# Feed-forward of layer 0: two of four hidden chunks get their outer convolution taps from VectorE, ScalarE and GpSimd in place of TensorE

## What is computed

```python
def bit_linear(x, w):                 # act_quant: rows to integers in -128..127 and back
    return einsum('bsd,hd->bsh', act_quant(x), weight_quant(w))   # weight_quant: -1, 0, 1 times a scale

h = bit_linear(layernorm(x), w1)      # 128 -> 512
h = depthwise_conv1d(h.transpose(0, 2, 1), conv_w, conv_b)   # 3 taps over the tokens, padding 1
h = silu(h.transpose(0, 2, 1))
x = x + bit_linear(h, w2)             # 512 -> 128, h is quantised again first
```

## Time and profile before

| | us |
|---|---|
| median of 3 runs | 563.39 |
| lowest and highest of them | 557.45, 567.11 |
| profiled execution, its own time | 562.17 |
| its span, first to last instruction | 560.4 |
| busy in the span: TensorE matmul | 476.8 |
| VectorE | 338.8 |
| ScalarE | 310.4 |
| GpSimd | 222.9 |

### The profile page before, as it was taken

How to read it: one execution, slowest core, us unless ns; L and a number is a source line. 1 busy time by engine, 2 the same in 40 slices (tenths; PEclk the granted TensorE clock), 3 DMA queues, 4 the chain that set the end, 5 groups by cost and what they waited for, 6 DMA issues and landing times.

```text
span 560.4 us, 12414 instructions
## 1 busy us (share of the span) xinstructions
PE 476.8 (85%) x3906; PEld 394.6 (70%) x3906; DVE 338.8 (60%) x1238; ACT 310.4 (55%) x676; POOL 222.9 (40%) x456
## 2 busy tenths in 40 slices
PE   3389898999998899958899999998999897499970
PEld 1277666776765788947877777776777597489970
DVE  6777677877782157677677787786868243022203
ACT  3137666777766445655866755665556563155540
POOL 7963322122313124445000125345254467745550
PEclk9989999999999999977999999999999998699995
DMA  6613333333407970034533333332210201322107
GB/s 177 191 43 110 90 115 105 111 92 95 125 3 303 424 235 2 10 119 136 172 120 97 92 106 118 103 111 83 92 55 8 74 20 34 91 66 70 49 15 225
DMA packets 52266, 60.05 MB, mean 107 GB/s; under 512 B 7633, under 2 KB 43354, under 8 KB 50928
## 3 DMA queue, kind: packets, MB, share of 16 engines
q1 hardware_dynamic: 46672, 52.73, 30.1%
q0 software_dynamic: 2272, 4.24, 2.3%
q10 hardware_dynamic: 3264, 2.36, 1.4%
HBM read 30.01 MB, written 29.23 MB: 106 GB/s over the span
## 4 chain that ended last, share of the span: by engine, by line
PE 51%; DVE 5%; DMA 4%; issue 3%; another core or an unknown queue 3%; ACT 2%; POOL 1%; DVEq 0%; SPq 0%; POOLq 0%
PE ps L1690 6%; PE ps L1639 6%; PE ps L1730 6%; PE ps L1733 5%; PE ps L1879 5%; PE ps L1889 5%; PE ps L1651 3%; PE ps L1653 2%; PE ps L1652 2%; ACT probs L996 1%; PE ps L1624 1%; DMA k_blocks<-y_dram 1%; PE ps L1940 1%; PE ps L1857 1%
## 5 line engine op out<-in xcount | busy, mean ns | idle before, releaser
L996 ACT ACTIVATE probs<-ps 128x512 f32<-128x512 f32 x256 | 147.4, 597 | 79.4 <-PE ps L1733 73.7
L1639 PE MATMUL ps<-k_blocks,q_stacks 128*128 128x256 f32 x512 | 118.5, 315 | 12.5 <-DMA k_blocks<-k_dram 6.6
L1268 DVE CUSTOM_DVE_ANT_0 ps<-ps,mask_q 128x256 f32<-128x256 f32 x256 | 102.5, 452 | 36.4 <-PE ps L1639 35.4
L1733 PE MATMUL ps<-q_stacks,k_blocks 128*128 128x256 f32 x512 | 105.3, 289 | 0.9 <-DMA q_stacks<-maxT 0.8
L1733 PEld LDWEIGHTS ps<-q_stacks,k_blocks 128*128 128x128 f32 x512 | 86.8, 189 | 20.8 <-issue 10.8
L1292 DVE TENSOR_REDUCE row_max<-ps 128x2 f32<-128x512 f32 x128 | 84.3, 687 | 27.5 <-PE ps L1639 26.2
L1639 PEld LDWEIGHTS ps<-k_blocks,q_stacks 128*128 128x128 f32 x512 | 80.2, 195 | 18.6 <-DMA k_blocks<-k_dram 5.3
L1690 PE MATMUL ps<-probs,v_aug 128*32 128x256 f32 x1024 | 68.5, 385 | 5.5 <-ACT probs L996 3.7
L796 POOL TENSOR_SCALAR max_split<-row_max 128x16 fp32r<-128x16 f32 x32 | 6.5, 204 | 156.7 <-issue 66.7
L1730 PE MATMUL ps<-mask_k,neg_mask_eye 128*128 128x512 f32 x128 | 54.5, 426 | 0.6 <-ACT experts L902 0.5
L741 POOL DMA_INDIRECT y_dram<-x_ring x39 | 40.8, 1046 | 28.4 <-ACT x_ring L1078 20.3
(11 more groups left out here) (221 smaller groups left out, 828.3 us busy)
## 6 DMA issues: line engine op xcount, KB each, us to landing
slots_dram<-x_ring SPq DMA_DIRECT2D x1, 10400.0 KB, 28.8
q_stacks<-q_dram SPq DMA_DIRECT2D x32, 256.0 KB
q_dram<-qk_parts SPq DMA_DIRECT2D x16, 384.0 KB, 3.7
k_dram<-qk_parts SPq DMA_DIRECT2D x16, 384.0 KB, 4.0
k_blocks<-k_dram SPq DMA_DIRECT2D x128, 48.0 KB
x_ring<-slots_dram SPq DMA_DIRECT2D x39, 65.0 KB
ctx_in<-ctx SPq DMA_DIRECT2D x16, 128.0 KB, 2.2
mask_in<-mask_Bx1xSxS_ik SPq DMA_DIRECT2D x8, 256.0 KB, 2.8
```

The source lines that it names most:

```text
L996: eng.activation(probs[:, n // HPS % 2, n % HPS, :, :].rearrange("p k q -> p (k q)"), ps[:, head_bank(BANKS_T, n)[0], :], ACT.Exp).then_in ...
L1268: last = eng.tensor_tensor_reduce(out=scored, in0=scored, in1=mask_q[t % 2][:, i, :], scale=1.0, scalar=-3.0e38, op0=ALU.add, op1=ALU.max, ...
L1639: mm = eng.matmul(ps[:, bank, i * S:(i + 1) * S], q_stack[r][:, st, i * P:(i + 1) * P], k_blocks[r][:, st, j, :], start=True, stop=True)
L1733: mm = eng.matmul(ps[:, bank, k * S:(k + 1) * S], k_blocks[r][:, st, j, k * P:(k + 1) * P], q_stack[r][:, st, :], start=(l == 0), stop=(l ...
```

## The change

For chunks 2 and 3 TensorE makes the middle product alone, with weights into which no tap is folded. Chunk 2 gets the middle tap by a scaled copy on ScalarE (`conv_middle`) and the outer taps by two multiply-and-adds on VectorE, straight from PSUM (`conv_sides`). Chunk 3 gets three scaled copies on ScalarE, one for each tap, and two additions on GpSimd (`conv_whole`). The SiLU is parted in two: chunks 0 and 1 as before, chunks 2 and 3 from SBUF behind both. The copies lie in the end of the `experts` tile, which is written only after the stage. On each engine:

- TensorE: chunks 2 and 3 of `ffn_hidden` have one product each, not three.
- ScalarE: `conv_middle` ahead of the first half of the SiLU, the second half behind `rounding(b)`.
- VectorE: `conv_sides(b+1)` between `quant_scale(b)` and `quant_clip(b)`.
- GpSimd: `conv_whole(0)` and `conv_whole(1)` between the last body of layer 0's attention and the tail; `conv_whole(b+2)` ahead of `ln_power(b)` in the loop.

Some semaphores are merged as well (`bo_ps`, `bo_new` and `x_biased` to `bo_sum`; `f_mean` into `f_stat`), with the same order of work; `h_act` counts two for each batch. The diff, cut to its core:

```diff
+    TAPPED = 2
+        conv_out = experts[:, E * EW - 4 * S:].rearrange("p (r c t) -> p r c t", r=2, c=2)
+        conv_side = experts[:, E * EW - 8 * S:E * EW - 4 * S].rearrange("p (r k t) -> p r k t", r=2, k=2)
...
+        def conv_whole(eng, b, r):
+
+            eng.wait_ge(h_mid, b + 1)
+            out, side = conv_out[:, r, 1, :], conv_side[:, r, :, :]
+            eng.tensor_tensor(out[:, 1:S], side[:, 0, 0:S - 1], out[:, 1:S], ALU.add).then_inc(h_side, 1)
+            eng.wait_ge(h_side, b * 2 + 1)
+            eng.tensor_tensor(out[:, 0:S - 1], side[:, 1, 1:S], out[:, 0:S - 1], ALU.add).then_inc(h_side, 1)
...
+            eng.tensor_copy(w1_taps[:, 1, TAPPED:FC, :], ffn_raw[:, 0, TAPPED:FC, :])
             for k in range(3):
-                for c in range(FC):
+                for c in range(TAPPED):
                     last = eng.tensor_scalar(w1_taps[:, k, c, :], ffn_raw[:, 0, c, :], conv_w[:, c, k:k + 1], None, ALU.mult)
...
             attention_gpsimd(eng, 0, "main 0", {-1: add_output_bias, 0: routing_constants})
+            conv_whole(eng, 0, 0)
+            conv_whole(eng, 1, 1)
             attention_gpsimd(eng, 0, "tail")
             attention_gpsimd(eng, 1, "head")
             for b in range(NB):
+                if exists(b + 2):
+                    conv_whole(eng, b + 2, b % 2)
                 ln_power(eng, ln_f0, b)
                 ln_apply(eng, ln_f0, b, bo[1])
...
+        def conv_middle(eng, b, r):
+
+            eng.wait_ge(h_ps, b * 2 + 2)
+            if after(b, 1):
+                eng.wait_ge(h_act, 2 * (b - 1))
+            eng.activation(conv_out[:, r, 0, :], hidden_ps(r, 2), ACT.Copy, scale=conv_w[:, 2, 1:2])
+            for k in range(2):
+                eng.activation(conv_side[:, r, k, :], hidden_ps(r, 3), ACT.Copy, scale=conv_w[:, 3, 2 * k:2 * k + 1])
+            eng.activation(conv_out[:, r, 1, :], hidden_ps(r, 3), ACT.Copy, scale=conv_w[:, 3, 1:2]).then_inc(h_mid, 1)
+
+        def conv_sides(eng, b, r):
+
+            eng.wait_ge(h_mid, b + 1)
+            chunks = (2,)
+            for c in chunks:
+                out, h = conv_out[:, r, c - 2, :], hidden_ps(r, c)
+                last = eng.scalar_tensor_tensor(out=out[:, 1:S], in0=h[:, 0:S - 1], scalar=conv_w[:, c, 0:1], in1=out[:, 1:S],
+                                                op0=ALU.mult, op1=ALU.add)
+            last.then_inc(h_conv, 1)
+            eng.wait_ge(h_conv, b * 2 + 1)
+            for c in chunks:
+                out, h = conv_out[:, r, c - 2, :], hidden_ps(r, c)
+                last = eng.scalar_tensor_tensor(out=out[:, 0:S - 1], in0=h[:, 1:S], scalar=conv_w[:, c, 2:3], in1=out[:, 0:S - 1],
+                                                op0=ALU.mult, op1=ALU.add)
+            last.then_inc(h_conv, 1)
+
+        def ffn_silu(eng, b, r, half):
             if after(b, 0):
                 eng.wait_ge(g_ps, b * NT)
-            for c in range(FC):
-                eng.wait_ge(h_ps, b * 2 + c // 2 + 1)
-                last = eng.activation(f_act[:, c, :], hidden_ps(r, c), ACT.Silu, bias=conv_b[:, c:c + 1])
+            if half == 0:
+                eng.wait_ge(h_ps, b * 2 + 1)
+                for c in range(TAPPED):
+                    last = eng.activation(f_act[:, c, :], hidden_ps(r, c), ACT.Silu, bias=conv_b[:, c:c + 1])
+            else:
+                eng.wait_ge(h_conv, b * 2 + 2)
+                eng.wait_ge(h_side, b * 2 + 2)
+                for c in range(TAPPED, FC):
+                    last = eng.activation(f_act[:, c, :], conv_out[:, r, c - TAPPED, :], ACT.Silu, bias=conv_b[:, c:c + 1])
             last.then_inc(h_act, 1)
...
                     if l == 0 and isinstance(b, int) and b == NB and n == 5:
                         eng.wait_ge(a.pv, NB * 4 - 1)
-                        ffn_silu(eng, 0, 0)
+                        conv_middle(eng, 0, 0)
+                        ffn_silu(eng, 0, 0, 0)
+                    if l == 0 and isinstance(b, int) and b == NB and n == 10:
+                        ffn_silu(eng, 0, 0, 1)
...
             def step(b, r):
                 if exists(b + 1):
-                    ffn_silu(eng, b + 1, 1 - r)
+                    conv_middle(eng, b + 1, 1 - r)
+                    ffn_silu(eng, b + 1, 1 - r, 0)
                 if exists(b - 1):
                     int_copy(b - 1)
                 if exists(b):
                     rounding(b)
+                if exists(b + 1):
+                    ffn_silu(eng, b + 1, 1 - r, 1)
                 if exists(b - 2):
                     xT_copy(b - 2)
...
+                    if l == 0 and isinstance(b, int) and b == NB and n == 6:
+                        conv_sides(eng, 0, 0)
...
+                quant_scale(b)
+                if exists(b + 1):
+                    conv_sides(eng, b + 1, 1 - r)
+                quant_clip(b)
...
             for c in range(2 * half, 2 * half + 2):
                 h = hidden_ps(r, c)
-                eng.matmul(h[:, :], w1T[:, 1, c, :], x, start=True, stop=False)
-                eng.matmul(h[:, 1:S], w1T[:, 0, c, :], x[:, 0:S - 1], start=False, stop=False)
-                mm = eng.matmul(h[:, 0:S - 1], w1T[:, 2, c, :], x[:, 1:S], start=False, stop=True)
+                if c >= TAPPED:
+                    mm = eng.matmul(h[:, :], w1T[:, 1, c, :], x, start=True, stop=True)
+                else:
+                    eng.matmul(h[:, :], w1T[:, 1, c, :], x, start=True, stop=False)
+                    eng.matmul(h[:, 1:S], w1T[:, 0, c, :], x[:, 0:S - 1], start=False, stop=False)
+                    mm = eng.matmul(h[:, 0:S - 1], w1T[:, 2, c, :], x[:, 1:S], start=False, stop=True)
...
-                for c in range(FC):
+                for c in range(TAPPED if k in (0, 2) else FC):
                     mm = eng.transpose(ps[:, bank, c * P:(c + 1) * P], w[:, c, :], ident[:, :])
...
-                eng.wait_ge(h_act, b + 1)
+                eng.wait_ge(h_act, 2 * (b + 1))
```

More of the change, by code:

```diff
@@ L332, in build @@
         h_ps, h_act = sem("h_ps"), sem("h_act")
+        h_mid, h_conv = sem("h_mid"), sem("h_conv")
+        h_side = sem("h_side")
         g_ps, g_stat, g_round, g_int = sem("g_ps"), sem("g_stat"), sem("g_round"), sem("g_int")
@@ L856, in add_output_bias @@
                 eng.wait_ge(ln_pre.xn, 3)
-                eng.wait_ge(bo_new, 2)
+                eng.wait_ge(bo_sum, 4)
                 eng.tensor_tensor(x_res[:, :, :], x_res[:, :, :],
-                                  bo[0][:, None, :].to_broadcast([P, NB * NT, D]), ALU.add).then_inc(x_biased, 1)
+                                  bo[0][:, None, :].to_broadcast([P, NB * NT, D]), ALU.add).then_inc(bo_sum, 1)
             def routing_constants():
@@ L1143, in ffn_scalar @@
             ffn_steps(eng, step, {1: lambda: attention_scalar(eng, 0, "tail")})
-            ffn_silu(eng, NB - 2, 0)
+            conv_middle(eng, NB - 2, 0)
+            ffn_silu(eng, NB - 2, 0, 0)
             int_copy(NB - 4)
@@ L1151, in ffn_scalar @@
             xT_copy(NB - 5)
-            ffn_silu(eng, NB - 1, 1)
+            conv_middle(eng, NB - 1, 1)
+            ffn_silu(eng, NB - 1, 1, 0)
             int_copy(NB - 3)
             rounding(NB - 2)
+            ffn_silu(eng, NB - 1, 1, 1)
             xT_copy(NB - 4)
@@ L1567, in _ @@
             eng.tensor_copy(ident_bf[:, :], ident[:, :])
-            eng.wait_ge(bo_ps, 2)
+            eng.wait_ge(bo_sum, 2)
             eng.wait_ge(bias_loaded, 6 * DMA)
             for l in range(2):
-                eng.tensor_tensor(bo[l][:, :], ps[:, BANKS_PRE["bo"], l * D:(l + 1) * D], bo[l][:, :], ALU.add).then_inc(bo_new, 1)
+                eng.tensor_tensor(bo[l][:, :], ps[:, BANKS_PRE["bo"], l * D:(l + 1) * D], bo[l][:, :], ALU.add).then_inc(bo_sum, 1)
             attention_vector(eng, 0, "main 0")
@@ L2084, in _ @@
             eng.wait_ge(f_stat, 2)
-            eng.matmul(ps[:, BANKS_PRE["mean"], 0:2], mean_ones[:, :], wq_stat[:, 0:2], start=True, stop=True).then_inc(f_mean, 1)
+            eng.matmul(ps[:, BANKS_PRE["mean"], 0:2], mean_ones[:, :], wq_stat[:, 0:2], start=True, stop=True).then_inc(f_stat, 1)
             eng.wait_ge(ln_pre.xn, 2)
@@ L2099, in _ @@
                 eng.matmul(ps[:, BANKS_PRE["bo"], l * D:(l + 1) * D], bv_wide[:, l, :], wo[l][:, :],
-                           start=True, stop=True).then_inc(bo_ps, 1)
+                           start=True, stop=True).then_inc(bo_sum, 1)
             eng.wait_ge(ln_pre.xs, 5)
```

27 lines of the change are left out of this document (11 added, 16 removed).

## The result

Six runs of the changed kernel have a median of 571.83 us (569.91 to 573.19), six of the kernel before 562.49; the ratio is 1.0174, 95% interval 1.0142 to 1.0205.

| runs | changed, us | before, us | ratio, 95% interval |
|---|---|---|---|
| first | 571.83 | 562.49 | 1.0174 [1.0142, 1.0205] |
| e7 | 570.87 | 562.40 | 1.0174 [1.0133, 1.0214] |
| e9 | 569.27 | 562.05 | 1.0131 [1.0085, 1.0178] |
| e15 | 569.39 | 563.39 | 1.0111 [1.0072, 1.0150] |

The account below looks back on a forecast made before the run. TensorE was taken to bound the feed-forward stage. From 562.17 us, plus 3.6 of lateness at the stage's end, less 0.3 in the prologue, came 565.5; one more clock fall of 0.8 made 566.3 us, range 560 to 571 (0.50).

Parts of the forecast that it names:

- What bounds the kernel: Feed-forward stage: TensorE is the bound, busy 7.00 of 7.00 us; the other engines have about 2 to 3 us of room.
- The start: Start of the feed-forward: batch 0's SiLU transposes 3.6 us late, because conv_whole(0) queues on GpSimd behind batch 7's ln_power.
- The clock behind the gap: Behind the 5.1 us TensorE idle stretch at the start: half clock for some 4 us, costing 1.7 us on the path.
- The tail: quantise_rows(7) stands behind conv_whole(1) on GpSimd, takes 3.0 us; batch 2's transposes come 3.3 us late.
- The steady steps: Feed-forward loop: first step 8.7 us, next two 14.1 together; 22.8 for three against 21.6 before, +1.2.
- one more fall: TensorE's idle pieces within the feed-forward steps bring one further drop to half clock, costing 0.8 us.
- Rival D: Feed-forward steps: the clock falls in most of them, 1.3 us a step, +6, 572.3 us; chance 0.12.
- Crowding: Feed-forward steps: VectorE's clips and GpSimd's work slow each other when side by side; 0.3 us allowed in the two-step loop.
- The end of the stage: Batch 5's lateness of 4.5, less 1.7, plus 0.8: low_parts 3.6 us late, and nothing behind gives that back.
- rival E: End of the feed-forward: no lateness reaches the end, since scores and experts' loads wait for transfers anyway; 562 us, chance 0.11.
- Rival B: Feed-forward steps: TensorE's relief counts, GpSimd's additions finish before wanted, ScalarE bounds steps at 6.0 us; 557.4 us, chance 0.13.
- Rival C: Feed-forward: GpSimd becomes the bound outright, additions 1.5 us each; +6, 572.3 us, chance 0.14.

Follow-up runs that it names:

- e7: The changed kernel run again, unaltered, beside the kernel before: 570.87 us against 562.40, ratio 1.0174.
- e9: The changed kernel run again, unaltered, as yardstick for runs beside it: 569.27 us against 562.05 for the kernel before, ratio 1.0131.
- e15: The changed kernel run once more, unaltered, as yardstick: 569.39 us against 563.39 for the kernel before, ratio 1.0111.
- e5: Against the kernel before: only chunk 3's outer taps moved to VectorE, three chunks kept as TensorE products, nothing on GpSimd; 558.79 us against 562.40, ratio 0.9953.
- e12: The changed kernel with GpSimd's first pair of additions moved ahead of batch 7's LayerNorm power: 565.27 us, ratio to the kernel before 1.0076.
- e11: The kernel before plus two pairs of GpSimd additions on spare memory, awaited by batches 0 and 1's SiLU: 568.76 us against 562.05, ratio 1.0104.
- e4: The changed kernel with TensorE's 5 us gap filled by repeating batch 6's row transposes 18 times: 570.60 us, ratio to the kernel before 1.0090.
- e10: The changed kernel with the start gap and the steps' gaps on TensorE filled by needless transposes: 567.39 us, ratio to the kernel before 1.0093.
- e1: The changed kernel with all of GpSimd's additions moved to VectorE: 563.02 us against 563.96 for the kernel before, ratio 0.9941.
- e3: The kernel before with 48 extra transposes (5.2 us) holding TensorE ahead of the first SiLU transposes: 569.32 us against 563.96, ratio 1.0086.
- e6: Against the kernel before: only chunk 3's taps moved to ScalarE copies and GpSimd additions, nothing new on VectorE; 567.23 us, ratio 1.0111.
- e2: The changed kernel with only batches 0 and 1's additions moved from GpSimd to VectorE: 564.71 us, ratio to the kernel before 1.0017.
- e13: The changed kernel with GpSimd's first pair of additions moved earlier and the steps' gaps filled by needless transposes: ratio to the kernel before 1.0008.

## Why the prediction came out half

Two steps of the prediction failed. It took 14.1 us for the two-step loop and 0.8 for all further falls of the clock, and the traces have 14.4 to 15.3 for that loop; with the tail this is 1.4 us. And it put what lies behind the stage at nothing ("nothing behind gives the 3.6 back"), where the profiles differ by 2.8 us, the cause of which stays open. The parts in order:

**What bounds the kernel: right.** TensorE was the bound of the stage before, and e5 shows what relief is worth while it stays so: its steps are shorter by the products that are gone.

**The start: right.** The place behind `ln_power` of batch 7 delayed the first transposes by 3.5 us (forecast 3.6), by way of a gap of 5.0 (5.1). e12 moves that pair alone and the lateness goes; e11 brings it into the kernel before and it comes. That it fits so well is in part luck: the first pair took 1.42 us from start to end where 1.8 were taken, and the hand-over and the SiLU behind it 1.0 where 0.8 were.

**The clock behind the gap: right.** 1.7 us, by e4 too. The clock was at half until 202.7, longer than the "some 4 us", but the work on the path meanwhile was the 1.7 us of the forecast. The Trainium skill ("TensorE: Matmul & The Clock Gate", HAM oscillation) has idle gaps cost the rate of the work behind them; the trace agrees with it at 196 us, and e10, where transposes to no purpose keep the clock at 1.00, shows it in the other direction.

**The tail: 0.7 short, 0.9 with what had come before it.** `quantise_rows` took 3.5 us, from 203.73 to 207.2, not 3.0; that is most of it.

**The steady steps: mis-sized, and over other work than forecast.** The step that failed is the sum's "14.1" for the two-step loop and, with it, the "one more fall" of 0.8. The first of the three steps came as forecast, 8.69 us (222.04 less 213.35; forecast 8.7). The two behind it took 15.32 (237.36 less 222.04); in the four profiles 15.3, 14.4, 15.3, 14.4. The forecast led the loop from the SiLU over the transposes (0.45) and VectorE's maxima and factors (1.9) to the rounding, and counted ScalarE's queue as a loop by itself (5.6). In e7, one of the shorter two, the chain is ScalarE's queue in that place: the copy of the rows, the change's four copies, the first SiLU half and the integer copy, 3.4 us and not 2.35.

```profile
221.84 0.27 ACT xnT_all L1182
222.10 0.36 ACT experts L913
...
224.29 0.97 ACT f_intT L1177 x2
225.27 1.17 ACT probs L1170 x2
```

LayerNorm was longer there as well (3.97 for 3.65), the additions shorter (1.65 for 1.8). The forecast's allowances, 0.5 for hand-overs and 0.6 for crowding and `conv_sides`, hid most of this, so that 14.1 came near 14.4 was in part luck. The two longer ones have a fall to half clock near their start, here from 223 to 226 us, behind an idle stretch of 2.98, and there the chain is TensorE's: its integer transposes and first product took 0.84 and 0.96 us in the chain above, and 0.45 and 0.49 at full clock two batches later.

```profile
223.00:224.00 1.00, 1.00 (x11) 1.00 (x9) 1.00 (x2) 1.00 (x4) 0.90 (x2) 0.51 0.00 0
...
226.00:227.00 1.00, 1.00 (x5) 0.84 (x4) 0.89 (x2) 0.57 (x1) 0.92 (x2) 0.78 0.00 0
```

So 0.3 of the 1.2 too little was the loop itself and 0.9 the fall, which the forecast had counted apart, at 0.8. Each of the four profiles has one or two such falls between 205 and 240 us, and not every gap brings one: e7's begins at 207 behind 1.43 us of idle time, and behind its 3.04 us at 218.8 the clock stays at 1.00; the same 1.43 us brought none in the profile above. The forecast's comparison with a single stretch could not tell which gap would bring one. The kernel before has no fall there in two profiles, and both kernels have falls behind 245. Rival D (falls in most steps) therefore fell. By e10 to `low_parts`, 60.0 us from the first product against 62.3 to 63.8 in the four profiles, all new falls together cost 2.3 to 3.8 us; the forecast had 1.7 and 0.8 for them.

**Crowding: right in kind.** The two clips stretch beside GpSimd's work. From the groups of VectorE's instructions between 190 and 245 us (line, tiles, count, busy us, mean ns): kernel before, changed kernel, and e1, where GpSimd does no additions.

```profile
L1475 DVE TENSOR_SCALAR f_int<-probs 128x512 bf16<-128x512 f32 x12 | 5.0, 461 | 0.0
```

```profile
L1536 DVE TENSOR_SCALAR f_int<-probs 128x512 bf16<-128x512 f32 x12 | 6.6, 586 | 0.0
```

```profile
L1533 DVE TENSOR_SCALAR f_int<-probs 128x512 bf16<-128x512 f32 x14 | 5.3, 417 | 0.0
```

One such clip of 128x512 takes 0.42 us undisturbed and up to 0.95 beside GpSimd's two-input additions: in the changed kernel the four clips of 0.85 to 0.95 us all ran beside L455, L768 or L770, while two beside the one-input instructions of `quantise_rows` took 0.42 and 0.52 (one-input work is not always harmless: in e5 a clip beside the mask conversion L784 took 0.85). In e1 no clip is stretched, but VectorE's own second addition (L770) takes 0.93 to 0.95 us the four times that it runs beside L455, and 0.42 the other four. The Trainium skill ("SBUF — State Buffer", SBUF: two separate sides) states a pair of ports that GpSimd shares with VectorE, where VectorE works in a two-port mode or with two inputs in SBUF, and that one instruction holds whole while the other waits. The doubling of single instructions, in place of a small slowing of all, agrees with it, but no run here shows in which mode the clip works, nor separates the port from other causes.

**The end of the stage: right.** It gave back 1.2 us between batch 5's transposes and `low_parts`, forecast 0.9, and from there nothing (rival E was wrong, as e3 shows).

**Behind the stage: 2.8 us that no step had, the largest piece of the error.** The sum stopped at the end of the stage ("nothing behind gives the 3.6 back"); that something behind could take more was not in it. Lateness alone does not do that: e3's 5.2 us cost 4.8. One difference is seen in the second half of the experts, where the clock is at half for longer in this profile (window of 17 us from about the same place: before, changed, and e9, the same kernel in another run):

```profile
481.00:498.00 17.00, 11.68 (x73) 10.97 (x73) 1.91 (x5) 4.45 (x13) 9.27 (x10) 0.70 0.30 82
```

```profile
487.00:504.00 17.00, 11.74 (x56) 11.17 (x57) 1.11 (x3) 3.50 (x11) 8.11 (x9) 0.53 0.26 71
```

```profile
487.00:504.00 17.00, 12.10 (x66) 11.65 (x67) 1.71 (x4) 4.32 (x12) 9.40 (x10) 0.70 0.30 77
```

In e9 the clock is as before, so the change doesn't force the fall; and e9's stretch from the first masked product to the end is 287.8 us, hardly less than the 288.0 of the profile with the lower clock, so this window doesn't explain the 2.8 us either. That stretch took 285.2 and 287.0 us in two profiles of the kernel before and 286.2 in e11; in the changed kernel 288.0, 290.0, 287.8 and 288.3; in the variants 286.1 (e6), 287.7 (e2), 288.7 (e10), 289.5 (e12), 290.6 (e4), and in e1, e5 and e13, whose stages are among the shortest, 291.3, 290.7 and 291.0. These are single executions, and some lie over the median of their kernel: e5's profile is of a run of 564.24 us, 5.4 over its median, which alone could cover its long stretch. So that the changed kernel is longer there than the kernel before, in all four profiles, is measured, its code being the same; why is open, and so is how much of it is the draw of the profiled run. Even the start of the stage, 183.1, 182.6, 182.1 and 181.7 us in the changed kernel, was 185.6 in e4, which has the same code up to there. The stage is the measure here that repeats best, to 1.2 and 1.4 us within each kernel.

**The account.** Of the 9.3 us by the first medians the forecast had 4.1. The 5.2 that are missing: the tail and the steps with their clock 1.4 (a stage 5.8 longer, forecast 3.6 and 0.8), behind the stage 2.8, the distance from this profile's difference (7.8) to that of the medians 1.5, less 0.5 that was gained ahead of the stage beyond the forecast's 0.3. By runs of whole kernels, which don't hang on one profile: the place of the first pair costs 0.55% (e9 to e12, 3.1 us, or 4.0 by the medians), the filled gaps give 0.3 to 0.7%, both together 1.03% (e15 to e13), and 0.1% is left, which is no difference within its interval of 0.35% either way. Rival B (relief counts) came true for TensorE's steps where the additions were off GpSimd, in e5 whole and in e1 in part. Rival C (GpSimd outright the bound) did not: its additions took 0.62 to 0.82 us, with one of 0.92 in the four profiles, and it was busy 61% at most in the steps.

## What to carry to other kernels

Work that is handed to an engine with room is handed to a place in its queue: look at which instruction stands ahead of it, what that one waits for, and move the new work up before you price it. Here two additions of 0.7 us each behind a wait cost 3 to 4 us against one place earlier, and 5.8 in a kernel that otherwise had no reason to wait (e11). When the bound engine is relieved and begins to idle in pieces, follow the new loop through every engine's queue, the relieved one's and the helpers' own new work included, and put a range for falls of TensorE's clock into the sum: here they cost 2.3 to 3.8 us in all, though only one or two of the gaps after the first brought one. And try the engine that looks too busy as well, since VectorE at 94% beat GpSimd at 61%.

## What was unexpected of the hardware

Keeping TensorE busy for nothing pays: twelve idle transposes a batch and 34 at the start (e10) took the clock from a mean of 0.91 to 1.00 over 60 us and the stage from 96.2 to 97.4 down to 93.7. GpSimd's addition of two operands shifted by one column costs no more than one in place: 0.625 to 0.816 and 0.722 to 0.785 us for 128x255, where L451 takes 0.722 to 0.934 for 128x256. VectorE's clips double their time beside additions on GpSimd that read two operands (0.85 to 0.95 us against 0.42). And the stretch of some 288 us behind the stage, whose code is the same in all these kernels, took from 285.2 to 291.3 us in the profiles: as much as the effects sought here. A stage cut out of the trace, beside the median of many runs, told apart what a single span could not.
